# Two cross-attentions over one context: low halves on other engines, more buffers, and four tiles turned by the DMA queue

## The chip, the cores and the metric

The kernel runs on one core of one Trainium2 chip, in one launch. The metric is device time in microseconds; the three runs of the kernel before have a median of 407.05 us (406.81 to 407.90). A profiled execution is one more run, with its own time. The core has five engines, each with its own queue of instructions: TensorE (PE; PEld is its weight load), VectorE (DVE), ScalarE (ACT), GpSimd (POOL) and SyncE (SP), which here issues nearly all DMAs. They meet at semaphores.

## The reference

Two layers on 64 tokens of 128 features. Each layer begins with cross-attention (16 heads of 64) to one shared context of 6272 tokens; then follow small blocks: self-attention and a mixture of 8 experts in the first layer, a delta rule with FIR filters and gates and a quantised feed-forward in the second. Cut to what matters here:

```
x = x + xattn0(layernorm(x), ctx, mask)    # attention 1: scores masked, softmax over 6272 keys
x = x + attn0(layernorm(x));  x = x + moe(layernorm(x))
y = layernorm(x)
out = y + attn(q=y, k=ctx, v=ctx)          # attention 2: the same context, no mask
x = x + attn(q=out, k=out, v=y)            # small
x = x + delta(layernorm(x));  x = x + ffn_quantised(layernorm(x))

attn(q, k, v) = softmax(q Wq (k Wk)^T / 8) (v Wv) Wo      # per head
```

## The kernel before

The weights of keys and values are folded into the query and the output, so both attentions work on the raw context. A tile is 128 rows (2 heads x 64 tokens) by 896 keys; there are 8 row tiles (RT) and 7 chunks of keys (CH), so 56 tiles (STEPS) in each attention, numbered n = 0 to 55 chunk by chunk. The softmax runs online: a running maximum, and the sums U and den are rescaled by alpha from chunk to chunk. Precision comes from halves: each f32 operand is split into an upper f16 and a low f16 (the rest), and a product is three f16 matmuls.

One tile passes through these stations:

- TensorE: scores, six matmuls (`score`, L490), into one of two pairs of PSUM banks.
- VectorE: the scaled, masked row maximum and the tile itself into `probs` (`maximum`, L641), one of 4 slots; slot n % 4 is free again when tile n - 4 has its low half (or has been turned by TensorE).
- ScalarE: the exponential with its row sums (`exps`, L559), then the upper half into a slot of `halves` (`upper`, L566). The upper half of tile n comes behind the exponential of tile n + 1.
- VectorE or GpSimd: the low half, `probs` minus upper half (`lower`, L594). `on_vector(L, n)` says which; L is 0 in attention 1 and 1 in attention 2.
- SyncE: a DMA transpose of both halves, 128 x 1792 f16, into a slot of `probsT` (`turn`, L421). It waits for the low half, and for the product of tile n - BUFS.
- TensorE: the product with the context, 21 matmuls (`pv`, L522), PV_LAG = 5 steps behind.
- VectorE: the sum into U (`add`, L654), ADD_LAG = 6 steps behind.

Some tiles take another way (`on_pe`): TensorE turns `probs` in f32 into PSUM (L502, 7 transposes), ScalarE copies the upper halves out (L573, L575) and VectorE the low ones (L661). Before, these are in attention 1 the tiles n % 4 = 3 from 7 on, and in both attentions tiles 51, 53, 54 and 55.

The order of the work is written out by hand, engine by engine. TensorE's step i is the scores of tile i + 2, a turn of tile i - 1 if that is its own, the product of tile i - 5. VectorE's step i is the maximum of tile i, the low half of tile i - 2 if that is VectorE's, the low half of a turned tile i - 3, and the sum of tile i - 6. GpSimd takes its low halves in order of n, and between them in attention 1 the next chunks of the context (scaled, split) and their mask, in attention 2 the quantisation of the feed-forward weights, one step every fourth tile from 12 to 40; and at n % 8 = 1 the running denominators. SyncE issues in order of n; in attention 1 a context transpose comes after every eighth tile (n % 8 = 3), and after the tiles named in WEIGHTS_AT a load of weights for later stages. SyncE issues in order: whatever waits in front holds up what is behind.

`dma_index` counts the tiles that go by DMA; their slot of `halves` is that index modulo HALF_BUFS, and each slot has a semaphore of its own. The tile `probsT` has BUFS slots, `halves` HALF_BUFS.

Of the kernel before, what the change touches and what calls it, by code (L numbers as in the profile page):

```python
# [19 lines left out]
P = 128  # L20
# [9 lines left out]
CK = TC * P  # L30
# [106 lines left out]
def build(nc, dram):  # L137
    with ExitStack() as ctx:
# [82 lines left out]
        probsT_parts = probsT[:].rearrange("p b k -> p (b k)").bitcast(F16).rearrange("p (b h k) -> p b h k", b=4, h=2)  # L221
        negmax = sb("negmax", [P, (CH + 1) * RT])
# [166 lines left out]
        def _(sp):  # L389
# [24 lines left out]
            def turn(L, n):  # L414

                if on_pe(L, n):
                    return
                sp.wait_ge(*lower_of(L, n))
                if n >= BUFS:
                    sp.wait_ge(sem("pv_done"), L * STEPS + n - BUFS + 1)  # L420
                sp.dma_start_transpose(probsT_parts[:, n % BUFS, :, :].rearrange("p h (k r) -> p (h k) r", r=P),  # L421
                                       halves_of(L, n).rearrange("p h k -> p (h k)")).then_inc(turned(L, n)[0], 16)
# [37 lines left out]
        def flash_pe(pe, L):  # L460
# [47 lines left out]
            def pv(n):  # L508
                c, b, bank = n // RT, n % BUFS, PV_BANKS[n % len(PV_BANKS)]
# [40 lines left out]
        def flash_act(act, L):  # L550
# [17 lines left out]
            def turned_upper(n):  # L568
                k = pe_index(L, n)
                act.wait_ge(sem("p_turned_lo"), k + 1)  # L570
                if n >= BUFS:
                    act.wait_ge(sem("pv_done"), base + n - BUFS + 1)
                act.copy(probsT_parts[:, n % BUFS, 0, 0:4 * P], ps[:, turn_banks(n)[0], :]).then_inc(sem("p_upper"), 1)  # L573
                act.wait_ge(sem("p_turned_hi"), k + 1)
                act.copy(probsT_parts[:, n % BUFS, 0, 4 * P:CK],  # L575
                         ps[:, turn_banks(n)[1], 0:CK - 4 * P]).then_inc(sem("p_upper"), 1)
# [43 lines left out]
        def flash_dve(dve, L, aside={}):  # L620
# [37 lines left out]
            def turned_lower(n):  # L658
                for part, (a, w) in enumerate(((0, 4 * P), (4 * P, CK - 4 * P))):
                    dve.wait_ge(sem("p_upper"), 2 * pe_index(L, n) + part + 1)  # L660
                    dve.tensor_tensor(probsT_parts[:, n % BUFS, 1, a:a + w], ps[:, turn_banks(n)[part], 0:w],  # L661
                                      probsT_parts[:, n % BUFS, 0, a:a + w], ALU.subtract).then_inc(sem("p_lower"), 1)
# [38 lines left out]
        def ctxT_first_dve(dve, half):  # L701

            dve.wait_ge(sem("ctxT_upper"), half + 1)
            keys = FIRST_KEYS[half]
            dve.scalar_tensor_tensor(ctxT_parts[:, CK + keys.start:CK + keys.stop], ctxT_raw[:, keys],
                                     ch_scale[:], ctxT_parts[:, keys], ALU.mult,
                                     ALU.subtract).then_inc(sem("ctxT_ready" if half else "ctxT_lower"), 1)

# [318 lines left out]
        def _(pe):  # L1027
# [39 lines left out]
            for half in range(2):  # L1067
                pe.wait_ge(sem("a_probs"), half + 1)
                for k in range(2):
# [6 lines left out]
            for half in range(2):  # L1076
                pe.wait_ge(sem("a_pcopied"), half + 1)
                for q in (half, 2 + half):
# [87 lines left out]
            for half in range(2):  # L1166
                pe.wait_ge(sem("b_probs"), half + 1)
                for k in range(2):
# [4 lines left out]
            for half in range(2):  # L1173
                pe.wait_ge(sem("b_pcopied"), half + 1)
                for a in range(2):
# [182 lines left out]
        def _(pool):  # L1358
# [129 lines left out]
        def _(act):  # L1488
# [19 lines left out]
            for half in range(2):  # L1508
                act.wait_ge(sem("a_max"), half + 1)
# [3 lines left out]
                ins.then_inc(sem("a_exp"), 1)  # L1513
            for half in range(2):
                act.wait_ge(sem("a_given"), A_GIVEN["pturned"] + half)
                act.copy(PT[:, 2 * half:2 * half + 2, :].rearrange("p j c -> p (j c)"),
                         ps[:, half, 0:2 * P]).then_inc(sem("a_pcopied"), 1)
            loaded(act, "par")
# [21 lines left out]
            for half in range(2):  # L1540
                act.wait_ge(sem("b_max"), half + 1)
# [3 lines left out]
                ins.then_inc(sem("b_exp"), 1)  # L1545
            for half in range(2):
                act.wait_ge(sem("b_pturned"), half + 1)
                act.copy(PT[:, 2 * half:2 * half + 2, :].rearrange("p j c -> p (j c)"),
                         ps[:, 4 + 3 * half, 0:2 * P]).then_inc(sem("b_pcopied"), 1)
            for half in range(2):  # L1550
# [49 lines left out]
        def _(dve):  # L1600
# [65 lines left out]
            for half in range(2):  # L1666
# [5 lines left out]
                seq(dve.scalar_tensor_tensor(sm2[:, rs, :], sm[:, rs, :], NEVER, sc, ALU.mult, ALU.add))  # L1672
                dve.tensor_reduce(smx[:, rs], sm2[:, rs, :], AX, ALU.max, negate=True).then_inc(sem("a_max"), 1)
            for half in range(2):
                rs = slice(4 * half, 4 * half + 4)
                dve.wait_ge(sem("a_exp"), half + 1)
                seq(dve.tensor_reduce(ssum[:, rs], sm[:, rs, :], AX, ALU.add))
                seq(dve.reciprocal(ssum[:, rs], ssum[:, rs]))
                dve.tensor_tensor(sm[:, rs, :], sm[:, rs, :], ssum[:, rs].unsqueeze(2).broadcast_to([P, 4, S]),
                                  ALU.mult).then_inc(sem("a_probs"), 1)  # L1680
            seq(dve.tensor_scalar(wamx[:], wamx[:], 1e-8, None, ALU.max))
# [94 lines left out]
            for half in range(2):  # L1776
                dve.wait_ge(sem("b_scores"), half + 1)
                dve.tensor_reduce(smx[:, 4 * half:4 * half + 4],
                                  ps[:, 3 - half, 0:4 * S].rearrange("p (h t) -> p h t", h=4), AX, ALU.max,
                                  negate=True).then_inc(sem("b_max"), 1)  # L1780
            for half in range(2):
                rs = slice(4 * half, 4 * half + 4)
                dve.wait_ge(sem("b_exp"), half + 1)
                seq(dve.tensor_reduce(ssum[:, rs], sm[:, rs, :], AX, ALU.add))
                seq(dve.reciprocal(ssum[:, rs], ssum[:, rs]))
                dve.tensor_tensor(sm[:, rs, :], sm[:, rs, :], ssum[:, rs].unsqueeze(2).broadcast_to([P, 4, S]),
                                  ALU.mult).then_inc(sem("b_probs"), 1)
            for half in range(2):
# [227 lines left out]
```

## Time and profile before

| | |
|---|---|
| median of three runs | 407.05 us |
| the profiled execution | 407.44 us, span 405.6 us, mean granted clock 0.995 |
| PE busy | 383.4 us (95%) |
| DVE, ACT busy | 286.4 us (71%), 287.9 us (71%) |
| POOL busy | 237.8 us (59%) |
| SyncE's DMA queue | 188048 packets, 66.77 MB, 81.7% of 16 engines |
| attention 1, attention 2 | about 19 to 172 us, about 210 to 351 us |

In the rows below L490 is a line of the kernel, `probsT<-halves` what is written and read, and x the count. A busy PE is a modelled one: matmuls are pipelined and the end of one lies behind the start of the next. The time in brackets is how long the engine stood idle before the row, and what ended that. SyncE's rows (SPq) are the issue of a DMA; its landing comes later. Times count from the start of the span.

### The profile page before, as it was taken

What the parts mean: (1) busy time and instruction counts of PE and PEld (TensorE: products, weight loads), DVE (VectorE), ACT (ScalarE), POOL (GpSimd) and SP (SyncE); (2) the same over time, 40 slices, a digit from 0 to 9 for tenths busy, and PEclk for the clock granted to TensorE, in tenths of its full rate; (3) what the DMA queues carried; (4) which work ended last, traced back from release to release, by engine and by line L of the source; (5) the groups of instructions that cost most, each with busy time, mean ns of one, the idle gap of its engine ahead of it and who ended that gap; (6) DMA issues with size and microseconds to landing.
All of it is one profiled execution on the core that took longest, in us unless ns stands there. A gap on an engine that the chain in (4) does not pass through costs nothing.

```text
span 405.6 us, 11389 instructions
## 1 busy us (share of the span) xinstructions
PE 383.4 (95%) x4529; PEld 280.3 (69%) x4529; DVE 286.4 (71%) x724; ACT 287.9 (71%) x568; POOL 237.8 (59%) x198
## 2 busy tenths in 40 slices
PE   7988999999998999989999999999999999999996
PEld 3435777777776778964955767777777778867843
DVE  2788888888875777556667767887887776445544
ACT  3477888888787887737429988899889987534240
POOL 2388989999974559301006997887787659030000
PEclk9899999999999999999999999999999999999999
DMA  8899998979989997990004999999999999700000
GB/s 307 321 257 193 178 179 136 178 143 210 238 179 212 190 210 137 331 410 34 3 2 90 193 192 194 193 201 192 206 170 210 183 206 185 284 2 2 4 1 5
DMA packets 188390, 68.56 MB, mean 169 GB/s; under 512 B 183200, under 2 KB 183984, under 8 KB 187440
## 3 DMA queue, kind: packets, MB, share of 16 engines
q1 hardware_dynamic: 188048, 66.77, 81.7%
q10 hardware_dynamic: 288, 1.05, 0.8%
q8 instruction: 36, 0.59, 0.6%
q14 instruction: 18, 0.15, 0.1%
HBM read 21.90 MB, written 0.03 MB: 54 GB/s over the span
## 4 chain that ended last, share of the span: by engine, by line
PE 52%; DVE 16%; DMA 10%; POOL 7%; ACT 6%; issue 6%; SPq 2%; POOLq 0%; DVEq 0%; ACTq 0%
PE ps L522 18%; PE ps L490 14%; DMA probsT<-halves 8%; DVE probs L641 7%; POOL halves L594 5%; PE ps L502 3%; ACT probs L559 2%; PE ps L1104 2%; PE ps L766 2%; SPq L421 2%; DMA moe<-in_ctxT 2%; ACT halves L566 1%; DVE U L654 1%; PE ps L1212 1%; PE ps L826 1%
## 5 line engine op out<-in xcount | busy, mean ns | idle before, releaser
L594 POOL TENSOR_TENSOR halves<-probs,halves 128x896 f16<-128x896 f32 x75 | 141.6, 1892 | 54.9 <-ACT halves L566 53.5
L522 PE MATMUL ps<-ctxN,probsT 128*128 128x128 f16 x2352 | 148.6, 219 | 4.6 <-DMA probsT<-halves 3.6
L522 PEld LDWEIGHTS ps<-ctxN,probsT 128*128 128x128 f16 x2352 | 139.4, 98 | 18.1 <-issue 8.0
L490 PE MATMUL ps<-ctxT_parts,GT_parts 128*128 128x512 f16 (+1 forms) x660 | 143.0, 353 | 5.4 <-DVE negmax L641 5.3
L559 ACT ACTIVATE probs<-probs,shifted 128x896 f32<-128x896 f32 x112 | 115.5, 1031 | 6.5 <-DVE shifted L646 6.5
L490 PEld LDWEIGHTS ps<-ctxT_parts,GT_parts 128*128 128x128 f16 x660 | 59.6, 98 | 57.0 <-DVE negmax L641 8.1
L566 ACT CAST halves<-probs 128x896 f16<-128x896 f32 x93 | 85.8, 923 | 0.1
L654 DVE SCALAR_TENSOR_TENSOR U<-U,alpha,ps 128x128 f32<-128x128 f32 x112 | 38.6, 345 | 54.4 <-PE ps L522 54.1
L641 DVE CUSTOM_DVE_ANT_0 probs<-ps,zero,negmax 128x896 f32<-128x896 f32 x56 | 67.5, 1205 | 1.7 <-POOL halves L594 1.2
L641 DVE CUSTOM_DVE_ANT_0 probs<-ps,maskb,negmax 128x896 f32<-128x896 f32 x56 | 67.5, 1205 | 1.6 <-issue 0.7
L556 ACT ACTIVATE alpha<-negmax 128x1 f32<-128x1 f32 x96 | 28.2, 294 | 37.0 <-DVE negmax L641 36.3
L766 PE MATMUL ps<-cst 128*128 128x512 f16 x135 | 34.8, 380 | 0.0
L594 DVE TENSOR_TENSOR halves<-probs,halves 128x896 f16<-128x896 f32 x18 | 24.0, 1336 | 0.7 <-ACT halves L566 0.7
L661 DVE TENSOR_TENSOR probsT<-ps,probsT 128x512 f16<-128x512 f32 (+1 forms) x38 | 21.8, 616 | 3.6 <-ACT probsT L573 3.6
L761 POOL TENSOR_TENSOR rstd<-mv,pows 128x1 f32<-128x1 f32 (+1 forms) x6 | 3.3, 546 | 35.1 <-DVE mv L745 24.1
L766 PEld LDWEIGHTS ps<-cst 128*128 128x128 f16 x135 | 13.0, 100 | 11.7 <-issue 0.9
L559 ACT ACTIVATION_READ_ACCUMULATOR probs<-probs,shifted 128x1 f32 x112 | 20.9, 187 | 0.0
L646 DVE TENSOR_SCALAR shifted<-negmax 128x1 f32<-128x1 f32 x112 | 17.2, 154 | 3.9
L502 PE MATMUL ps<-cst,probs 128*128 128x128 f32 x133 | 17.3, 273 | 0.0
L1385 POOL TENSOR_SCALAR maskb<-moe 128x896 bf16<-128x896 int32 x5 | 16.1, 3217 | 0.4
L502 PEld LDWEIGHTS ps<-cst,probs 128*128 128x128 f32 x133 | 15.3, 141 | 1.1
L1483 POOL TENSOR_TENSOR orn<-oms,pows 128x2 f32<-128x2 f32 x1 | 0.7, 698 | 23.3 <-DVE oms L1909 23.3
(369 smaller groups left out, 380.3 us busy)
## 6 DMA issues: line engine op xcount, KB each, us to landing
moe<-in_ctxT SPq DMA_DIRECT2D x7, 448.0 KB, 7.6
moe<-in_mask SPq DMA_DIRECT2D x6, 448.0 KB, 10.0
moe<-in_gateT SPq DMA_DIRECT2D x2, 1024.0 KB, 9.2
moe<-in_upT SPq DMA_DIRECT2D x2, 1024.0 KB, 10.9
moe<-in_downT SPq DMA_DIRECT2D x2, 1024.0 KB, 12.8
moe<-in_fir_long SPq DMA_DIRECT2D x1, 2048.0 KB, 10.3
probsT<-halves SPq DMA_TRANSPOSE x93, 4.6
wv<-in_wv SPq DMA_DIRECT2D x2, 512.0 KB, 6.9
```

What stands on the lines that cost most here:

```text
L490: ins = pe.matmul(ps[:, 2 * b + h, 0:width], GT_parts[:, g_part, r * P:(r + 1) * P], ctxT_parts[:, keys:keys + width], start=(g_part == 0 ...
L502: ins = pe.transpose(ps[:, turn_banks(n)[t // 4], t % 4 * P:(t % 4 + 1) * P], probs[:, n % BUFS, t * P:(t + 1) * P], ident)
L522: ins = pe.matmul(ps[:, bank, 0:D], probsT_parts[:, b, p_part, k * P:(k + 1) * P], ctxN_parts[:, at:at + D], start=(p_part == 0 and c_part ...
L556: act.activation(alpha[:, n:n + 1], negmax[:, n:n + 1], ACT.Exp, bias=negmax[:, n + RT:n + RT + 1], scale=-1.0)
L559: act.activation(probs[:, n % BUFS, :], probs[:, n % BUFS, :], ACT.Exp, bias=shifted[:, n:n + 1], scale=-1.0, accum_out=chunksum[:, n:n + ...
L566: act.copy(halves_of(L, n)[:, 0, :], probs[:, n % BUFS, :]).then_inc(sem("upper_done"), 1)
L594: eng.tensor_tensor(halves_of(L, n)[:, 1, :], probs[:, n % BUFS, :], halves_of(L, n)[:, 0, :], ALU.subtract).then_inc(lower_of(L, n)[0], 1)
L641: dve.tensor_tensor_reduce(out=probs[:, n % BUFS, :], in0=scored, in1=added, scale=descale[:, L:L + 1], scalar=negmax[:, n:n + 1], op0=ALU ...
L646: dve.tensor_scalar(shifted[:, n:n + 1], negmax[:, n + RT:n + RT + 1], PROB_LOG, None, ALU.add).then_inc(sem("shifted"), 1)
L654: dve.scalar_tensor_tensor(U[:, r, :], U[:, r, :], alpha[:, n:n + 1], ps[:, PV_BANKS[n % len(PV_BANKS)], 0:D], ALU.mult, ALU.add).then_inc ...
L661: dve.tensor_tensor(probsT_parts[:, n % BUFS, 1, a:a + w], ps[:, turn_banks(n)[part], 0:w], probsT_parts[:, n % BUFS, 0, a:a + w], ALU.sub ...
L766: pe.matmul(ps[:, bank, :], ident.bitcast(F16)[:, 0:P], cst[:, 0:2 * P].bitcast(F16), start=True, stop=True)
```

## The change

Of the fifteen tiles that TensorE turns in attention 1, four (35, 39, 43 and 47) now go by DMA. In attention 1 VectorE makes the low halves of tile 0 and of n % 4 = 1 up to 33 (tile 2 goes to GpSimd, tile 33 comes from it), and from tile 5 on one step later than before: behind the maximum of tile n + 3 instead of n + 2. In attention 2 all low halves are GpSimd's; before, nine were VectorE's (n % 4 = 3 from 15 to 47). `probsT` has 6 slots instead of 4, `halves` 7 instead of 5; the room comes from a descriptor scratch of 1024 bytes in place of the default. Loads of weights stand at other tiles. Semaphores of two small blocks are shared (a_... and b_... become s_..., the second block counting on), and one unused increment goes.

```diff
-BUFS, HALF_BUFS = 4, 5
+BUFS, TURNED_BUFS, HALF_BUFS = 4, 6, 7
-RAMP = 12
...
-        probsT = sb("probsT", [P, BUFS, CK])
+        probsT = sb("probsT", [P, TURNED_BUFS, CK])
...
-        WEIGHTS_AT = {24: ("in1", w_qT, "wqT1"), 27: ("in1", wkT[:], "wkT1"), 30: ("out0", wv[:], "wv0"),
-                      33: ("out0", wo[:], "wo0"), 36: ("ffn", win[:], "win"), 38: ("ffn", wout[:], "wout"),
-                      40: ("small_attn", a_w[:], "a_w"), 42: ("delta", d_w[:], "d_w"), 44: ("delta", w1s[:], "w1s")}
+        WEIGHTS_AT = {14: ("in1", w_qT, "wqT1"), 22: ("in1", wkT[:], "wkT1"), 30: ("out0", wv[:], "wv0"),
+                      34: ("small_attn", a_w[:], "a_w"), 36: ("ffn", win[:], "win"), 38: ("out0", wo[:], "wo0"),
+                      40: ("ffn", wout[:], "wout"), 44: ("delta", d_w[:], "d_w"), 46: ("delta", w1s[:], "w1s")}
 
         def on_pe(L, n):
-            return L == 0 and n % 4 == 3 and n > 4 or n >= STEPS - 3 or n == STEPS - 5
+            return L == 0 and n % 4 == 3 and 4 < n < 33 or n >= STEPS - 3 or n == STEPS - 5
 
         def on_vector(L, n):
             if L == 0:
-                return n in (0, 2) or 4 <= n < 30 and n % 4 == 1
-            return n >= RAMP and n % 4 == 3
+                return n == 0 or 4 <= n < 34 and n % 4 == 1
+            return False
...
-                if n >= BUFS:
-                    sp.wait_ge(sem("pv_done"), L * STEPS + n - BUFS + 1)
+                if n >= TURNED_BUFS:
+                    sp.wait_ge(sem("pv_done"), L * STEPS + n - TURNED_BUFS + 1)
...
-                if 2 <= i < STEPS + 2 and on_vector(L, i - 2) and not on_pe(L, i - 2):
-                    lower(dve, L, i - 2)
+                done = i - (2 if L or i <= 4 else 3)
+                if (0 if L or i <= 4 else BUFS) <= done < STEPS and on_vector(L, done) and not on_pe(L, done):
+                    lower(dve, L, done)
...
-    nc = bacc.Bacc("TRN2", target_bir_lowering=False, num_devices=1)
+    nc = bacc.Bacc("TRN2", target_bir_lowering=False, num_devices=1, dynamic_dma_scratch_size=1024)
```

## Rows read from the trace of the kernel before

**Rows 1.** The page: span, SyncE's queue, and a transpose's issue to landing (last column, us).
```profile
span 405.6 us, 11389 instructions
...
q1 hardware_dynamic: 188048, 66.77, 81.7%
...
probsT<-halves SPq DMA_TRANSPOSE x93, 4.6
```
**Rows 2.** Stages: length, busy PE, PEld, DVE, ACT, POOL, PEclk, DMA share, GB/s.
```profile
117.22:149.80 32.58, 30.78 (x358) 24.04 (x356) 23.27 (x57) 26.61 (x55) 18.25 (x12) 1.00 1.17 211
224.24:336.11 111.87, 109.49 (x1266) 82.15 (x1265) 86.47 (x197) 99.62 (x187) 88.02 (x65) 1.00 1.17 195
```
**Rows 3.** TensorE's order in attention 1: start, us, instruction, count, [idle before].
```profile
108.43 1.30 PE L490 MATMUL ps<-ctxT_parts,GT_parts 128*128 128x512 f16 x6
...
110.74 1.30 PE L490 MATMUL ps<-ctxT_parts,GT_parts 128*128 128x512 f16 x6
...
123.83 1.33 PE L522 MATMUL ps<-ctxN,probsT 128*128 128x128 f16 x21 [1.80 <-DMA probsT<-halves]
125.00 1.30 PE L490 MATMUL ps<-ctxT_parts,GT_parts 128*128 128x512 f16 x6
...
128.07 1.30 PE L490 MATMUL ps<-ctxT_parts,GT_parts 128*128 128x512 f16 x6
...
162.71 1.70 PE L502 MATMUL ps<-cst,probs 128*128 128x128 f32 x14
```
**Rows 4.** Waits of TensorE, 36-105, 105-160, 211-352 us: us, times, longest.
```profile
PE ps L490 <- DVE negmax L641: 2.3, 5, 1.0
...
PE ps L522 <- DMA probsT<-halves: 1.8, 1, 1.8
...
PE ps L522 <- DMA probsT<-halves: 1.8, 5, 0.6
...
PE ps L490 <- DVE negmax L641: 0.4, 1, 0.4
```
**Rows 5.** SyncE's order in attention 1: start, us of the issue.
```profile
115.61 1.10 SPq L391 DMA_DIRECT2D wo<-in_wo  x1
117.22 1.56 SPq L421 DMA_TRANSPOSE probsT<-halves  x1
118.82 3.21 SPq L411 DMA_TRANSPOSE ctxN<-ctxT_parts  x1
122.13 2.99 SPq L421 DMA_TRANSPOSE probsT<-halves  x1
```
**Rows 6.** Issues in attention 2, 224 to 336.2 us: ns min/median/max, first and last.
```profile
L421 SPq DMA_TRANSPOSE probsT<-halves x48: 1297/2094/3612, 224.2 to 336.1; - x48
```
**Rows 7.** GpSimd's order in attention 2.
```profile
220.45 9.35 POOL L594 TENSOR_TENSOR halves<-probs,halves 128x896 f16<-128x896 f32 x5 [1.00 <-ACT halves L566]
...
251.75 1.90 POOL L594 TENSOR_TENSOR halves<-probs,halves 128x896 f16<-128x896 f32 x1 [2.51 <-ACT halves L566]
...
255.64 1.89 POOL L594 TENSOR_TENSOR halves<-probs,halves 128x896 f16<-128x896 f32 x1
```
**Rows 8.** Two short stretches of attention 2, columns as in rows 2.
```profile
218.75:220.50 1.75, 1.75 (x10) 0.87 (x9) 1.55 (x4) 1.75 (x4) 0.75 (x2) 1.00 1.13 214
...
239.50:241.00 1.50, 1.50 (x25) 1.33 (x23) 0.91 (x3) 0.71 (x2) 1.50 (x2) 1.00 1.26 280
```
**Rows 9.** GpSimd's and VectorE's order before tile 34's issue.
```profile
108.82 3.22 POOL L1385 TENSOR_SCALAR maskb<-UT 128x896 bf16<-128x896 int32 x1
112.11 1.90 POOL L594 TENSOR_TENSOR halves<-probs,halves 128x896 f16<-128x896 f32 x1
...
111.20 1.21 DVE L641 CUSTOM_DVE_ANT_0 probs<-ps,maskb,negmax 128x896 f32<-128x896 f32 x1
```
**Rows 10.** VectorE's low halves, both attentions: ns min/median/max, first and last.
```profile
L594 DVE TENSOR_TENSOR halves<-probs,halves x18: 1080/1106/2581, 26.2 to 325.5; 128x896 f16<-128x896 f32 x18
```
**Rows 11.** Waits of SyncE, 205 to 355 us.
```profile
SPq L420 <- PE ps L522: 0.2, 1, 0.2
```

More of the change, by code:

```diff
@@ L218, in build @@
         scrap = probs[:, 2:4, :].rearrange("p b k -> p (b k)")
-        probsT = sb("probsT", [P, BUFS, CK])
+        probsT = sb("probsT", [P, TURNED_BUFS, CK])
         halves = sb("halves", [P, HALF_BUFS, 2, CK], F16)
-        probsT_parts = probsT[:].rearrange("p b k -> p (b k)").bitcast(F16).rearrange("p (b h k) -> p b h k", b=4, h=2)
+        probsT_parts = probsT[:].rearrange("p b k -> p (b k)").bitcast(F16).rearrange("p (b h k) -> p b h k", b=TURNED_BUFS,
+                                                                                      h=2)
         negmax = sb("negmax", [P, (CH + 1) * RT])
@@ L418, in turn @@
                 sp.wait_ge(*lower_of(L, n))
[L419 to L421 removed]
+                if n >= TURNED_BUFS:
+                    sp.wait_ge(sem("pv_done"), L * STEPS + n - TURNED_BUFS + 1)
+                sp.dma_start_transpose(probsT_parts[:, n % TURNED_BUFS, :, :].rearrange("p h (k r) -> p (h k) r", r=P),
                                        halves_of(L, n).rearrange("p h k -> p (h k)")).then_inc(turned(L, n)[0], 16)
@@ L508, in pv @@
             def pv(n):
-                c, b, bank = n // RT, n % BUFS, PV_BANKS[n % len(PV_BANKS)]
+                c, b, bank = n // RT, n % TURNED_BUFS, PV_BANKS[n % len(PV_BANKS)]
                 if L == 0 and n % RT == 0:
@@ L570, in turned_upper @@
                 act.wait_ge(sem("p_turned_lo"), k + 1)
-                if n >= BUFS:
-                    act.wait_ge(sem("pv_done"), base + n - BUFS + 1)
-                act.copy(probsT_parts[:, n % BUFS, 0, 0:4 * P], ps[:, turn_banks(n)[0], :]).then_inc(sem("p_upper"), 1)
+                if n >= TURNED_BUFS:
+                    act.wait_ge(sem("pv_done"), base + n - TURNED_BUFS + 1)
+                act.copy(probsT_parts[:, n % TURNED_BUFS, 0, 0:4 * P], ps[:, turn_banks(n)[0], :]).then_inc(sem("p_upper"), 1)
                 act.wait_ge(sem("p_turned_hi"), k + 1)
-                act.copy(probsT_parts[:, n % BUFS, 0, 4 * P:CK],
+                act.copy(probsT_parts[:, n % TURNED_BUFS, 0, 4 * P:CK],
                          ps[:, turn_banks(n)[1], 0:CK - 4 * P]).then_inc(sem("p_upper"), 1)
@@ L660, in turned_lower @@
                     dve.wait_ge(sem("p_upper"), 2 * pe_index(L, n) + part + 1)
-                    dve.tensor_tensor(probsT_parts[:, n % BUFS, 1, a:a + w], ps[:, turn_banks(n)[part], 0:w],
-                                      probsT_parts[:, n % BUFS, 0, a:a + w], ALU.subtract).then_inc(sem("p_lower"), 1)
+                    dve.tensor_tensor(probsT_parts[:, n % TURNED_BUFS, 1, a:a + w], ps[:, turn_banks(n)[part], 0:w],
+                                      probsT_parts[:, n % TURNED_BUFS, 0, a:a + w], ALU.subtract).then_inc(sem("p_lower"), 1)
             for i in range(STEPS + ADD_LAG):
@@ L704, in ctxT_first_dve @@
             keys = FIRST_KEYS[half]
-            dve.scalar_tensor_tensor(ctxT_parts[:, CK + keys.start:CK + keys.stop], ctxT_raw[:, keys],
-                                     ch_scale[:], ctxT_parts[:, keys], ALU.mult,
-                                     ALU.subtract).then_inc(sem("ctxT_ready" if half else "ctxT_lower"), 1)
+            ins = dve.scalar_tensor_tensor(ctxT_parts[:, CK + keys.start:CK + keys.stop], ctxT_raw[:, keys],
+                                           ch_scale[:], ctxT_parts[:, keys], ALU.mult, ALU.subtract)
+            if half:
+                ins.then_inc(sem("ctxT_ready"), 1)
         def bound_dve(dve, seq, L, total):
@@ L1067, in _ @@
             for half in range(2):
-                pe.wait_ge(sem("a_probs"), half + 1)
+                pe.wait_ge(sem("s_probs"), half + 1)
                 for k in range(2):
@@ L1076, in _ @@
             for half in range(2):
-                pe.wait_ge(sem("a_pcopied"), half + 1)
+                pe.wait_ge(sem("s_pcopied"), half + 1)
                 for q in (half, 2 + half):
@@ L1166, in _ @@
             for half in range(2):
-                pe.wait_ge(sem("b_probs"), half + 1)
+                pe.wait_ge(sem("s_probs"), half + 3)
                 for k in range(2):
@@ L1173, in _ @@
             for half in range(2):
-                pe.wait_ge(sem("b_pcopied"), half + 1)
+                pe.wait_ge(sem("s_pcopied"), half + 3)
                 for a in range(2):
@@ L1452, in _ @@
                     pool.wait_ge(sem("u_turned"), 3)
-                    pool.wait_ge(sem("a_max"), 2)
+                    pool.wait_ge(sem("s_max"), 2)
                     pool.memset(den[:], 0.0).then_inc(sem("cleared"), 1)
@@ L1508, in _ @@
             for half in range(2):
-                act.wait_ge(sem("a_max"), half + 1)
+                act.wait_ge(sem("s_max"), half + 1)
                 for k in range(4):
@@ L1512, in _ @@
                     ins = act.activation(sm[:, r, :], sm2[:, r, :], ACT.Exp, bias=smx[:, r:r + 1])
-                ins.then_inc(sem("a_exp"), 1)
+                ins.then_inc(sem("s_exp"), 1)
             for half in range(2):
@@ L1516, in _ @@
                 act.copy(PT[:, 2 * half:2 * half + 2, :].rearrange("p j c -> p (j c)"),
-                         ps[:, half, 0:2 * P]).then_inc(sem("a_pcopied"), 1)
+                         ps[:, half, 0:2 * P]).then_inc(sem("s_pcopied"), 1)
             loaded(act, "par")
@@ L1540, in _ @@
             for half in range(2):
-                act.wait_ge(sem("b_max"), half + 1)
+                act.wait_ge(sem("s_max"), half + 3)
                 for k in range(RT // 2):
@@ L1544, in _ @@
                     ins = act.activation(sm[:, r, :], ps[:, 3 - half, k * S:(k + 1) * S], ACT.Exp, bias=smx[:, r:r + 1])
-                ins.then_inc(sem("b_exp"), 1)
+                ins.then_inc(sem("s_exp"), 1)
             for half in range(2):
@@ L1548, in _ @@
                 act.copy(PT[:, 2 * half:2 * half + 2, :].rearrange("p j c -> p (j c)"),
-                         ps[:, 4 + 3 * half, 0:2 * P]).then_inc(sem("b_pcopied"), 1)
+                         ps[:, 4 + 3 * half, 0:2 * P]).then_inc(sem("s_pcopied"), 1)
             for half in range(2):
@@ L1672, in _ @@
                 seq(dve.scalar_tensor_tensor(sm2[:, rs, :], sm[:, rs, :], NEVER, sc, ALU.mult, ALU.add))
-                dve.tensor_reduce(smx[:, rs], sm2[:, rs, :], AX, ALU.max, negate=True).then_inc(sem("a_max"), 1)
+                dve.tensor_reduce(smx[:, rs], sm2[:, rs, :], AX, ALU.max, negate=True).then_inc(sem("s_max"), 1)
             for half in range(2):
                 rs = slice(4 * half, 4 * half + 4)
-                dve.wait_ge(sem("a_exp"), half + 1)
+                dve.wait_ge(sem("s_exp"), half + 1)
                 seq(dve.tensor_reduce(ssum[:, rs], sm[:, rs, :], AX, ALU.add))
@@ L1679, in _ @@
                 dve.tensor_tensor(sm[:, rs, :], sm[:, rs, :], ssum[:, rs].unsqueeze(2).broadcast_to([P, 4, S]),
-                                  ALU.mult).then_inc(sem("a_probs"), 1)
+                                  ALU.mult).then_inc(sem("s_probs"), 1)
             seq(dve.tensor_scalar(wamx[:], wamx[:], 1e-8, None, ALU.max))
@@ L1779, in _ @@
                                   ps[:, 3 - half, 0:4 * S].rearrange("p (h t) -> p h t", h=4), AX, ALU.max,
-                                  negate=True).then_inc(sem("b_max"), 1)
+                                  negate=True).then_inc(sem("s_max"), 1)
             for half in range(2):
                 rs = slice(4 * half, 4 * half + 4)
-                dve.wait_ge(sem("b_exp"), half + 1)
+                dve.wait_ge(sem("s_exp"), half + 3)
                 seq(dve.tensor_reduce(ssum[:, rs], sm[:, rs, :], AX, ALU.add))
@@ L1786, in _ @@
                 dve.tensor_tensor(sm[:, rs, :], sm[:, rs, :], ssum[:, rs].unsqueeze(2).broadcast_to([P, 4, S]),
-                                  ALU.mult).then_inc(sem("b_probs"), 1)
+                                  ALU.mult).then_inc(sem("s_probs"), 1)
             for half in range(2):
```

## The prediction

> **What bounds the kernel now.** I read the page first, then the stages, then TensorE's and the DMA queue's own order, then the waits. The page [rows 1] has a span of 405.6 us, of which SyncE's queue, which carries nearly all transfers, fills 82% of the 16 engines. The stages [rows 2] show where: in attention 2 (224 to 336 us) and in 117 to 150 us of attention 1 the queue's share is 1.17, above 1 since packets overlap. The granted clock is 1.00 in both (the upper level, 2.4 GHz), so nothing is lost there. In TensorE's order [rows 3] a step is 2.31 us (108.43 to 110.74: the scores of one tile and the product of another), and 3.07 us when TensorE turns a tile as well (125.00 to 128.07); a turn is 0.77 us. The stage is TensorE's wherever nothing else is late, and the reader is to see what is late in the waits [rows 4]: in attention 1 VectorE's row maximum up to 105 us (five waits), then one late DMA tile, 1.80 us before 123.83 [rows 3]; in attention 2 almost only late DMA tiles. The queue's order [rows 5] shows why: from tile 34's issue at 117.22 on, each issue begins 0.04 to 0.1 us after the one before has ended. In attention 2 there are 48 issues from 224.2 to 336.1 [rows 6], one per (336.1 - 224.2) / 47 = 2.38 us, at the pace of TensorE. So two things bound attention in turns, TensorE and the queue, and the change takes work from the first and gives it to the second.
>
> **The change, part by part.** All sums are made against the profiled execution, 407.44 us, of which 405.6 are the span; the median of the runs, 407.05, lies 0.39 lower.
>
> *Four turns leave TensorE* (tiles 35, 39, 43 and 47 of attention 1). TensorE loses 4 x 0.77 = 3.1 us. ScalarE's two copies and VectorE's two subtractions for each go too; neither engine releases TensorE in that stretch [rows 4], so I count nothing. GpSimd gets four low halves of 1.87 us (9.35 us for five in a row, [rows 7]); behind tile 34 it has 2.31 us per tile and little else, so they are hidden.
>
> *The queue gets four tiles*, each 128 x 1792 two-byte elements, 0.459 MB. What it does from tile 34's issue on, before: ten tiles, two context transposes and five loads in 32.6 us (117.22 to 149.8), without a pause [rows 2, 5]. After: the same, three more tiles (35, 39, 43) up to the issue of tile 47, and the load of wo0, which moves from tile 33 to tile 38 and takes 1.10 us to issue [rows 5]; then tiles 47 to 49 until tile 50 is issued. With t for a tile more in a full queue that is 32.6 + 1.1 + 6t. Bounds for t: 0.459 MB at 280 GB/s, the best rate of a stretch, is 1.6 us, and at the 195 GB/s of all of attention 2 it is 2.35 us; one transpose alone runs at 214 GB/s, 2.1 us [rows 2, 8]. That is the nearest row; as a backlog can speed it up, I take 2.0. To the issue of tile 50: 45.7 us. Landing is 4.6 us after the issue [rows 1], 0.1 until TensorE starts and 1.2 for the product: 51.6 us from tile 34's issue to the end of tile 50's product. Before, that product ends where the turns of tiles 53 and 54 begin, at 162.71: 162.71 - 117.22 = 45.5 us [rows 3, 5]. So this stretch grows by 6.1 us (3.7 to 8.2). TensorE alone would want, from product to product, 16 x 2.31 + 0.77 = 37.7 us; the queue wants about 8 us more, and the 3.1 us saved are lost in waits.
>
> The Trainium skill, "DMA: Bandwidth & Descriptors", section "Latency and other measured facts", gives a DMA transpose an effective 261 GB/s. Nineteen transposes and 1.64 MB of loads are 10.4 MB, 39.7 us by that figure as an estimate, against 49 us at the 211 GB/s of rows 2; by the page the queue would hold TensorE by some 2 us and not 8, and the first rival would win. The trace has a rate like it only in short stretches [rows 8].
>
> *Low halves one step later in attention 1* (VectorE's tiles, n % 4 = 1). They move from the step before a turn into the one with the turn, which is 0.77 us longer. The five waits for the maximum, 2.3 us [rows 4], mostly go; a modelled end lies 0.16 us behind the next start (123.83 + 1.33 against 125.00, [rows 3]), so from start to start they are 3.1 us. The longest, 1.0 + 0.16 near tile 8, I count as given back: tile 2's low half goes to GpSimd, behind a mask conversion like that of 3.22 us in rows 9, and the issues of tiles 2, 3 and 4 move back with it. That leaves 1.9; I take 1.7 us (0.8 to 3.1), and by so much tile 34's step comes earlier. A tile's low half lands about 2 us later in the queue; the tiles have more than that in hand up to tile 32, where the queue is not full.
>
> *Where tile 34's issue comes.* Before, at 117.22: a mask, then the low half of tile 33 on GpSimd at 112.11 and of tile 34 behind it, then wo0 [rows 5, 9]. After: tile 33's low half is VectorE's, behind the maximum of tile 36, which began at 111.20 [rows 9] and now 1.7 earlier, at 109.5; it ends 1.4 later, the subtraction takes 1.1 to 2.6 us [rows 10], since GpSimd starts tile 34's at the same moment; tile 33's issue of 1.5 us follows. Tile 34 is issued at 113.6 to 115.1; I take the middle, 2.9 earlier than before. Attention 1 so ends 6.1 - 2.9 = 3.2 us later. Bounds: 3.7 - 2.9 - 0.8 = 0 and 8.2 - 2.0 = 6.2.
>
> *All low halves on GpSimd in attention 2.* VectorE loses nine, and the one wait of 0.4 us for the maximum [rows 4] goes. GpSimd, tiles 12 to 43: 32 x 1.87 = 59.8; eight steps of the weight quantisation, each pushing the next low half back by 1.0 to 2.1 us (255.64 - 251.75 = 3.89, so 2.0 more, [rows 7]; all eight 12.4); four running denominators, 2.0, one copy, 0.8. Sum 75.0 us, against 32 x 2.31 = 73.9 for TensorE. So GpSimd becomes as tight as the other two. Its lag is largest, about 3.3 us, behind the second weight's third step (tile 37). A low half may be late by 1.5 us before the maximum four tiles on waits for it, and that by 0.6 before TensorE does: up to 1.2 us in all, less what TensorE loses anyway on late DMA tiles (1.8 us, rows 4), in which GpSimd catches up. I take +0.7, with the 0.4 gained +0.3 (-0.6 to +2.0).
>
> *Deeper buffers.* In attention 2 the queue's waits on the product four tiles back sum to 0.2 us, once [rows 11]; what it waits for there is the low half. So six and seven slots instead of four and five give 0 (0 to 0.2). A tile whose low half is late gains nothing by a free slot.
>
> *The smaller descriptor scratch* makes room for them. Every transpose here is issued by SyncE. No row shows what the scratch does. The Trainium skill, "DMA: Bandwidth & Descriptors", section "SWDGE vs HWDGE vs iDMA", says that the rings in that carveout serve DMAs issued by GpSimd and that SyncE's path does not touch them; no run here shows it. I take 0. The merged semaphores and the dropped increment change no order: 0. Loads: wqT1 and wkT1 move to tiles 14 and 22, where the queue has pauses: 0, and it costs about 1 us of issue each if that cover is gone.
>
> Sum: 405.6 + 3.2 + 0.3 = 409.1 us of span; with the 1.84 us around it 410.9, and by the 0.39 of the median 410.5 us.
>
> **Rivals.**
> 1. *The queue has room (faster).* If a full queue runs at its best rate (280 GB/s, rows 8) for longer, each of 19 transposes takes 1.6 us, the loads hide among them, and TensorE bounds attention 1: from tile 34's product to tile 50's 37.7 us, which starts 5 steps after the step at 108.43 - 1.7. Product 50 would end at 158.3 instead of 162.71, -4.4, and with +0.3 the time is 403.0. For it: the rate has been seen, and before 117 us the queue paused. Against it: the 32.6 us in which it never paused ran at 211 GB/s.
> 2. *Balance.* t is 1.6 and tile 34 comes early (113.6): 3.7 - 2.9 - 0.8 = 0 in attention 1, and 407.3 in all.
> 3. *GpSimd bounds attention 2.* Attention 1 even, but the lag of 3.3 us meets the late DMA tiles instead of hiding in them: 1.2 us and 0.2 more for each of the five waits, less 0.4: +1.8, 408.9.
> 4. *It doesn't do what it says:* the smaller scratch slows every transpose. At the longest issue seen, 3.6 us [rows 6], instead of 2.1, 97 transposes cost over 100 us.
>
> **How the numbers follow.** Forecast 0.48; rival 1 0.25; rival 2 0.17; rival 3 0.07; rival 4 0.03. A run of this kernel can tell 0.3%, 1.2 us. Faster (below 405.8) is rival 1: 0.25. Same is rival 2: 0.17. Slower is the forecast with rivals 3 and 4: 0.58. The forecast alone runs from 408.3 to 413. The range of 8 in 10 reaches into rival 1 until half of it is left out, 404.5, and up to 413.0.
>
> **What would show it.** After: late DMA tiles as TensorE's largest wait between 118 and 162 us, some 8 us, where there was one of 1.8; SyncE's issues without a pause from tile 34 to tile 50, tile 50 issued near 160; 4 x 7 transposes fewer at L502; no wait of TensorE for the maximum up to 105 us but the first. In attention 2 no low half on VectorE, GpSimd without a pause between tiles 16 and 44, late DMA tiles about as before. I am wrong if the issues of tiles 34 to 50 follow each other in under 2.2 us on the mean, loads included, or if attention 2 changes by more than 2 us.

## The result and the profile after

The changed kernel takes 415.74 us (median of 4 runs, 415.21 to 416.06), against 407.48 for the kernel before, run beside it: ratio 1.0198, 95% interval 1.0177 to 1.0219. It is slower, as forecast, but by 8.3 us where 3.4 were forecast, and it lies above the range (404.5 to 413.0). The profiled execution took 415.80.

The page of the changed kernel: the span, TensorE's turns, the DMA queue, and the transposes' issue to landing.
```profile
span 413.7 us, 11323 instructions
...
L502 PE MATMUL ps<-cst,probs 128*128 128x128 f32 x105 | 13.6, 273 | 0.0
...
q1 hardware_dynamic: 195344, 68.61, 83.1%
...
probsT<-halves SPq DMA_TRANSPOSE x97, 4.8
```
105 transposes on TensorE are 15 tiles, four fewer than before, and the queue has 97 transposes instead of 93 [rows 1]. So the change does what it says.

SyncE's order in the changed kernel, from tile 34's issue on, and the issues of tiles 44 and 50 (columns as in [rows 5], the last one a count):
```profile
115.94 1.78 SPq L421 DMA_TRANSPOSE probsT<-halves  x1
117.77 1.08 SPq L391 DMA_DIRECT2D a_w<-in_a_w  x1
119.36 1.92 SPq L421 DMA_TRANSPOSE probsT<-halves  x1
121.34 2.66 SPq L411 DMA_TRANSPOSE ctxN<-ctxT_parts  x1
124.10 1.56 SPq L421 DMA_TRANSPOSE probsT<-halves  x1
...
126.88 3.89 SPq L421 DMA_TRANSPOSE probsT<-halves  x2
130.83 1.06 SPq L391 DMA_DIRECT2D wo<-in_wo  x1
131.98 5.25 SPq L421 DMA_TRANSPOSE probsT<-halves  x2
...
147.52 3.31 SPq L421 DMA_TRANSPOSE probsT<-halves  x1
...
163.28 5.32 SPq L421 DMA_TRANSPOSE probsT<-halves  x2
```
Up to tile 50 each issue follows the one before within 0.15 us, but for the 0.51 behind the first load. Tile 34 is issued at 115.94 (117.22 before, [rows 5]) and tile 50 at 163.28.

TensorE's order in the changed kernel: three early waits, the scores of tile 36 and the end of product 50 as in [rows 3], and the longest wait between them.
```profile
35.39 1.31 PE L490 MATMUL ps<-ctxT_parts,GT_parts 128*128 128x512 f16 x6 [1.63 <-DVE negmax L641]
...
44.84 1.33 PE L522 MATMUL ps<-ctxN,probsT 128*128 128x128 f16 x21 [0.46 <-DMA probsT<-halves]
...
48.10 1.33 PE L522 MATMUL ps<-ctxN,probsT 128*128 128x128 f16 x21 [0.79 <-DMA probsT<-halves]
...
108.08 1.30 PE L490 MATMUL ps<-ctxT_parts,GT_parts 128*128 128x512 f16 x6
...
139.18 1.53 PE L522 MATMUL ps<-ctxN,probsT 128*128 128x128 f16 x21 [3.08 <-DMA probsT<-halves]
...
169.64 1.70 PE L502 MATMUL ps<-cst,probs 128*128 128x128 f32 x14
```
The row at 108.08 (the scores of tile 36) stood at 108.43 before; the turns of tiles 53 and 54, which begin when the product of tile 50 ends, stand at 169.64 instead of 162.71: 6.9 us later. That is most of the 8.1 us that the span grew by.

TensorE's waits in the changed kernel (us, times, longest), from 28 to 120, 120 to 178 and 218 to 360 us:
```profile
PE ps L490 <- DVE negmax L641: 2.7, 3, 1.6
PE ps L522 <- DMA probsT<-halves: 1.8, 3, 0.8
...
PE ps L522 <- DMA probsT<-halves: 8.4, 8, 3.1
...
PE ps L522 <- DMA probsT<-halves: 4.1, 10, 0.8
PE ps L490 <- DVE GT_parts L881: 0.2, 1, 0.2
```
Against [rows 4]: late DMA tiles cost 8.4 us in the second half of attention 1, where there was one wait of 1.8; and the first half has waits of its own. In attention 2 they cost 4.1 instead of 1.8.

It is the queue that is late there, and not GpSimd, which now makes the low halves of all these tiles. GpSimd's row for tile 44's low half:
```profile
138.75 1.88 POOL L594 TENSOR_TENSOR halves<-probs,halves 128x896 f16<-128x896 f32 x1 [0.43 <-ACT halves L566]
```
It ends at 140.63, and SyncE issues tile 44 at 147.52. From tile 35 to tile 50 each low half ends 1.6 to 7.2 us before its tile is issued. The stretch of the full queue, columns as in [rows 2]:
```profile
115.94:163.28 47.34, 40.49 (x441) 29.48 (x440) 26.27 (x65) 34.70 (x66) 33.49 (x26) 0.96 1.13 209
```
The transposes of attention 2, as in [rows 6]:
```profile
L421 SPq DMA_TRANSPOSE probsT<-halves x48: 1342/2033/3833, 230.9 to 343.8; - x48
```
The rate is 209 GB/s where it was 211. In attention 2 the 48 issues span 112.8 us instead of 111.9.

### The profile page after: what moved, and what is told of

It is laid out like the page before. It is cut to its first block, busy times and chain, and to the rows that moved or that the text cites. A ratio compares the mean times of both kernels' runs of the same rounds, so it can differ in the third digit from the quotient of the medians.

```text
span 413.7 us, 11323 instructions
## 1 busy us (share of the span) xinstructions
PE 382.5 (92%) x4501; PEld 277.0 (67%) x4501; DVE 273.1 (66%) x707; ACT 287.8 (70%) x564; POOL 263.8 (64%) x211
## 4 chain that ended last, share of the span: by engine, by line
PE 44%; POOL 15%; DMA 15%; DVE 10%; ACT 7%; issue 5%; SPq 2%; POOLq 0%; DVEq 0%; ACTq 0%
PE ps L522 16%; DMA probsT<-halves 13%; PE ps L490 12%; POOL halves L594 11%; DVE probs L641 3%; ACT probs L559 2%; DMA moe<-in_ctxT 2%; ACT halves L566 2%; PE ps L1106 2%; PE ps L502 2%; PE ps L768 2%; PE ps L1214 1%; PE ps L828 1%; PE ps L942 1%; DVE halves L594 1%
## 5 line engine op out<-in xcount | busy, mean ns | idle before, releaser
L594 POOL TENSOR_TENSOR halves<-probs,halves 128x896 f16<-128x896 f32 x88 | 168.3, 1922 | 34.5 <-ACT halves L566 33.2
L566 ACT CAST halves<-probs 128x896 f16<-128x896 f32 x97 | 89.5, 923 | 0.1
L661 DVE TENSOR_TENSOR probsT<-ps,probsT 128x512 f16<-128x512 f32 (+1 forms) x30 | 17.3, 618 | 6.1 <-ACT probsT L573 6.1
L502 PE MATMUL ps<-cst,probs 128*128 128x128 f32 x105 | 13.6, 273 | 0.0
L594 DVE TENSOR_TENSOR halves<-probs,halves 128x896 f16<-128x896 f32 x9 | 12.8, 1419 | 0.0
L502 PEld LDWEIGHTS ps<-cst,probs 128*128 128x128 f32 x105 | 12.0, 141 | 0.8
```

Source lines behind the costliest of these rows:

```text
L502: ins = pe.transpose(ps[:, turn_banks(n)[t // 4], t % 4 * P:(t % 4 + 1) * P], probs[:, n % BUFS, t * P:(t + 1) * P], ident)
L566: act.copy(halves_of(L, n)[:, 0, :], probs[:, n % BUFS, :]).then_inc(sem("upper_done"), 1)
L594: eng.tensor_tensor(halves_of(L, n)[:, 1, :], probs[:, n % BUFS, :], halves_of(L, n)[:, 0, :], ALU.subtract).then_inc(lower_of(L, n)[0], 1)
L661: dve.tensor_tensor(probsT_parts[:, n % TURNED_BUFS, 1, a:a + w], ps[:, turn_banks(n)[part], 0:w], probsT_parts[:, n % TURNED_BUFS, 0, a:a ...
```

## The experiments

**Which part costs.** Four kernels, each one part undone or one part alone.

a_turns_back: the changed kernel with TensorE's tiles as before.
```diff
-            return L == 0 and n % 4 == 3 and 4 < n < 33 or n >= STEPS - 3 or n == STEPS - 5
+            return L == 0 and n % 4 == 3 and n > 4 or n >= STEPS - 3 or n == STEPS - 5
```


> The changed kernel, but TensorE turns tiles 35, 39, 43 and 47 of attention 1 again. Theory Q (the queue is full from tile 34 to tile 50 and each of the four tiles costs it some 2.3 us): the 8.4 us that TensorE waits for late DMA tiles between 120 and 178 us fall under 2, the product of tile 50 ends near 161.5 us instead of 169.7, attention 2 keeps its 1.4 us more, and the time is 407.3 us (before: 407.5; changed: 415.7). Rival S (every transpose became slower through the smaller scratch, the more slots or the moved loads): the late tiles stay, four turns of 0.77 us come on top, and the time is 412 us or more.

Measured: 406.95 us, ratio to before 0.9984 (0.9967 to 1.0). No late DMA tile from 105 us to the end of attention 1; product 50 ends at:
```profile
160.75 1.70 PE L502 MATMUL ps<-cst,probs 128*128 128x128 f32 x14
```

b_four_only: the kernel before with that one line as in the changed kernel (the diff above, read backwards).

> The kernel before, but tiles 35, 39, 43 and 47 of attention 1 go by DMA; nothing else of the change. Theory Q: from tile 34's issue at 117.2 us the queue takes 32.6 + 6 x 2.27 = 46.2 us to the issue of tile 50, whose product ends near 169.3 us, 6.6 later than before: 414.1 us. Rival S (the four tiles fit, and it is the scratch, the slots or the loads that cost): 406 to 408.5 us.

Measured: 415.55 us, 1.0199 (1.0171 to 1.0227); late DMA tiles, 115 to 178 us, and the end of product 50:
```profile
PE ps L522 <- DMA probsT<-halves: 7.1, 5, 2.4
```
```profile
169.04 1.16 PE L502 MATMUL ps<-cst,probs 128*128 128x128 f32 x9
```
The four tiles alone make the whole difference, and taking them back takes the whole difference away. Rival S falls: from tile 34's issue (116.95) to tile 50's (162.99) b needs 46.0 us with four and five slots, the default scratch and five loads; the changed kernel needs 47.3 with six and seven slots, the small scratch and six loads.

c_att2_vector and d_att1_lows_back: the changed kernel with the low halves of attention 2, or those of attention 1, as before.
```diff
 c:
-            return False
+            return n >= 12 and n % 4 == 3
 d:
-                return n == 0 or 4 <= n < 34 and n % 4 == 1
+                return n in (0, 2) or 4 <= n < 30 and n % 4 == 1
...
-                done = i - (2 if L or i <= 4 else 3)
-                if (0 if L or i <= 4 else BUFS) <= done < STEPS and on_vector(L, done) and not on_pe(L, done):
+                done = i - 2
+                if 0 <= done < STEPS and on_vector(L, done) and not on_pe(L, done):
```


> The changed kernel, but VectorE makes nine low halves of attention 2 again (n % 4 = 3 from 15 to 47). Theory G (GpSimd as the only maker of low halves leaves the queue waiting, which costs the 1.4 us by which attention 2 grew): the last product of attention 2 starts 140.0 us after its first scores, as before, and not 141.3; time 414.4 us. Rival I (the 1.4 us are an accident of which transposes fall on a pause of the queue): still about 141.3, time 415.7 us.

> The changed kernel, but the low halves of attention 1 are made as before: tiles 0, 2 and n % 4 = 1 from 5 to 29 by VectorE, tile 33 by GpSimd, none a step later. Theory L (the later low halves are what brought tile 34's issue forward from 117.2 to 115.9 us, and it decides when the full queue starts): tile 34 is issued near 117.2 again, time 417.0 us. Rival E (what the new assignment costs at the start, 4.2 us of waits up to step 15 where there were 1.6, with tiles 2 to 5 late, is more than it gives): tile 34 is issued at 115 or before, time 413.5 to 415 us.

Measured: c 416.06 us (1.0212, 1.0185 to 1.0239), though its attention 2 took 140.1 us from first scores to last product, as G expected; d 416.26 us (1.0214, 1.0188 to 1.0241), with tile 34 issued at 116.18. Neither gain nor loss shows in the times: G is not borne out, and L and E both miss. The moved loads alone give d's start (116.24 in g_loads_only below), so next to nothing of the changed kernel's earlier start comes from its low halves. That they neither gained nor lost in sum asked for the run on tile 2 below.

**What a tile and a load cost the full queue.** e_loads_later and h_two_tiles, both on the changed kernel (the last two lines of e stand behind the loop over the tiles of attention 1):
```diff
 e:
...
-                      34: ("small_attn", a_w[:], "a_w"), 36: ("ffn", win[:], "win"), 38: ("out0", wo[:], "wo0"),
-                      40: ("ffn", wout[:], "wout"), 44: ("delta", d_w[:], "d_w"), 46: ("delta", w1s[:], "w1s")}
+        WEIGHTS_LAST = [("out0", wo[:], "wo0"), ("small_attn", a_w[:], "a_w"), ("ffn", win[:], "win"),
+                        ("ffn", wout[:], "wout"), ("delta", d_w[:], "d_w"), ("delta", w1s[:], "w1s")]
...
+            for name, t, src in WEIGHTS_LAST:
+                load(name, t, src)
 h:
-            return L == 0 and n % 4 == 3 and 4 < n < 33 or n >= STEPS - 3 or n == STEPS - 5
+            return L == 0 and n % 4 == 3 and 4 < n < 41 or n >= STEPS - 3 or n == STEPS - 5
```


> The changed kernel, but the six loads of weights that stand behind tiles 34 to 46 of attention 1 come behind all its tiles. Theory Q (in the full queue everything costs by its bytes: a transpose some 2.28 us, a load about 1.05): from tile 34's issue to tile 50's 18 transposes remain, 18 x 2.28 = 41.0 us instead of 47.3; the product of tile 50 ends near 163.4 us instead of 169.7, and the time is 409.4 us. Rival W (loads ride in gaps between the transposes for nothing, and a transpose costs 47.3 / 18 = 2.6 us): 47 us as before, 415.5 us. By the 2.0 us a tile of the prediction it would be 36 us, TensorE would bound, and 406 us come out.

> The changed kernel, but TensorE turns tiles 35 and 39 again; 43 and 47 stay with the DMA queue. Theory Q (full queue, 2.28 us a tile): 47.3 - 4.6 = 42.8 us from tile 34's issue to tile 50's, product 50 ends near 165 us, time 411 us, half-way between 407.0 with four turns back and 415.7. Rival T (the queue has room for two tiles, and it only tips over with four): 406.5 to 408 us.

Measured: e 411.09 us (1.0076, 1.0049 to 1.0103). SyncE's order in e, between the issues of tiles 34 and 50, and the rate of that stretch:
```profile
116.50 3.72 SPq L421 DMA_TRANSPOSE probsT<-halves  x2
120.27 3.61 SPq L411 DMA_TRANSPOSE ctxN<-ctxT_parts  x1
123.99 17.75 SPq L421 DMA_TRANSPOSE probsT<-halves  x8
141.79 2.19 SPq L411 DMA_TRANSPOSE ctxN<-ctxT_parts  x1
144.07 14.30 SPq L421 DMA_TRANSPOSE probsT<-halves  x6
```
```profile
116.50:158.46 41.96, 37.93 (x435) 28.07 (x433) 25.84 (x64) 33.88 (x65) 33.24 (x26) 1.00 1.17 196
```
18 transposes in 41.96 us, nothing between them: 2.33 us each, and TensorE still waits for late tiles. The six loads cost 47.34 - 41.96 = 5.4 us, 0.9 each (by the times 4.7, 0.8 each); theory W falls. e comes out 1.7 us above what Q expected: 1.0 in this stretch, the rest in a later start and in attention 2.

h: 410.99 us (1.0081, 1.006 to 1.0101), where Q expected 411 and T at most 408: two tiles cost 4.0 us above a_turns_back, and two more 4.8. The queue has no room for even two. But in its profile the stretch took 45.4 us, not 42.8. In the five profiles with all four tiles and the loads between them (the changed kernel, b, c, d, i) it took 46.0 to 47.6, so by the stretch two tiles fewer take off 1 to 2 us where Q has 4.6. Only the times agree with Q; why the stretch does not stays open.

**Where the earlier start went.** i_tile2_back: the changed kernel with tile 2's low half by VectorE.
```diff
-                return n == 0 or 4 <= n < 34 and n % 4 == 1
+                return n in (0, 2) or 4 <= n < 34 and n % 4 == 1
```


> The changed kernel with one low half moved back: tile 2 of attention 1 by VectorE. Theory M (tile 2's low half behind GpSimd's first mask is what ate the gain of the later low halves, so that the full queue starts only at 115.9 us): the scores of tile 36 start near 106.2 us instead of 108.1, tile 34 is issued near 114 us, the product of tile 50 ends near 167.7 us, and the time is 413.7 us. Rival K (before tile 34 the queue is already so late that an earlier TensorE gains nothing): 415.5 us.

Measured: 412.98 us (1.0145, 1.0122 to 1.0168): by this one low half 2.8 us less than the changed kernel, or 2.2 by the two ratios, each to the kernel before run beside it. TensorE's order in i:
```profile
32.81 1.31 PE L490 MATMUL ps<-ctxT_parts,GT_parts 128*128 128x512 f16 x6 [1.14 <-DVE negmax L641]
...
105.52 1.30 PE L490 MATMUL ps<-ctxT_parts,GT_parts 128*128 128x512 f16 x6
...
165.95 1.70 PE L502 MATMUL ps<-cst,probs 128*128 128x128 f32 x14
```
The scores of tile 36 start at 105.52, 2.6 us before those of the changed kernel, tile 34 is issued at 112.98, 3.0 before, and product 50 ends 3.7 earlier. Other profiles bear it out: with tile 2 on VectorE these scores start at 105.3 to 106.2 (i, and f, j and k below; l, whose attention 1 began late, is left aside), with tile 2 on GpSimd at 108.1 to 108.6 (the changed kernel, a, c, e, h). What tile 2 does there is in the changed kernel's GpSimd and VectorE:
```profile
28.79 3.22 POOL L1387 TENSOR_SCALAR maskb<-moe 128x896 bf16<-128x896 int32 x1
32.09 5.58 POOL L594 TENSOR_TENSOR halves<-probs,halves 128x896 f16<-128x896 f32 x3
```
```profile
34.12 1.21 DVE L641 CUSTOM_DVE_ANT_0 probs<-ps,maskb,negmax 128x896 f32<-128x896 f32 x1 [3.09 <-POOL halves L594]
```
Tile 2's low half waits for the mask conversion, and tiles 3 and 4 come behind it. VectorE's maximum of tile 6 needs the slot of tile 2 and stands 3.09 us; TensorE loses 1.63 for it, and 0.46 and 0.79 for the late transposes of tiles 4 and 5 (rows of TensorE above).

g_loads_only: the kernel before with the loads at the changed places.

> The kernel before with the loads of weights at the changed places, nothing else. Theory O (wo0 in front of tile 34 made its DMA late, 1.96 us of TensorE's wait): tile 34 is issued 1.1 us earlier, the wait falls under 0.9 us, time 406.3 us. Rival N (a load moved behind tile 38 makes a later tile late by as much): 407.5 us.

Measured: 406.50 us, 0.9979 (0.9965 to 0.9993). Tile 34 is issued at 116.24, one wait for a late tile is left between 110 and 178 us:
```profile
PE ps L522 <- DMA probsT<-halves: 0.6, 1, 0.6
```
The moved loads are worth about 1 us, and with wo0 out of its way tile 34 is issued 1.0 earlier, as O expected.

**What is good in the change, and the version that beats both.** f_parts is a_turns_back with c's line and i's line; j_gpsimd_att2 is f without c's line; k_few_slots is f with the slots and the scratch of before:
```diff
 k:
-BUFS, TURNED_BUFS, HALF_BUFS = 4, 6, 7
+BUFS, TURNED_BUFS, HALF_BUFS = 4, 4, 5
...
-    nc = bacc.Bacc("TRN2", target_bir_lowering=False, num_devices=1, dynamic_dma_scratch_size=1024)
+    nc = bacc.Bacc("TRN2", target_bir_lowering=False, num_devices=1)
```


> The changed kernel with three parts undone: TensorE turns all its tiles again, VectorE makes nine low halves of attention 2 again, and that of tile 2 of attention 1. Theory R (what is left, later low halves from tile 5 on, the moved loads and more slots, gains, and the two low-half assignments lose): the scores of tile 36 start near 106.5 us instead of 108.1, attention 2 takes 140.2 us instead of 141.0, and the time is 404.5 us. Rival Z (the early waits only move, as with the other assignment, and attention 2's difference is within its scatter): 406.5 to 407 us.

> The same kernel as f_parts, beside the two that each differ from it in one part: 404.7 us.

> f_parts, but all low halves of attention 2 are GpSimd's. Theory G (GpSimd alone is as tight as the queue there and starves it now and then): 0.8 us more than f_parts, 405.5 us; the last product starts 141.1 us after the first scores of attention 2 instead of 140.3. Rival I (scatter): 404.7 us.

> f_parts with four slots of probsT, five of halves and the default descriptor scratch, as before. Theory N (more slots and the smaller scratch do nothing, since the queue waits for low halves and not for slots): 404.7 us. Rival D (with four slots the queue waits for products in attention 1, some 11 us in 8 waits before, and a late tile stays late): 405.5 to 406.5 us.

| | us (range) | ratio to before |
|---|---|---|
| f_parts | 404.74 (403.98 to 405.37) | 0.9931 (0.9905 to 0.9957) |
| l_parts_again | 405.13 (403.94 to 408.29) | 0.9935 (0.9914 to 0.9957) |
| j_gpsimd_att2 | 404.65 (403.63 to 404.97) | 0.9931 (0.991 to 0.9952) |
| k_few_slots | 404.12 (403.32 to 405.34) | 0.9921 (0.9898 to 0.9943) |

The highest run, l's 408.29, is its profiled execution, in which TensorE's granted clock over the first 20 us was 0.74 (0.91 in f's); its attention 1 began 3.3 us later. In f the scores of tile 36 start at 106.16 and product 50 ends at 158.50, with no late DMA tile in between (the row between them is the product of tile 34):
```profile
106.16 1.30 PE L490 MATMUL ps<-ctxT_parts,GT_parts 128*128 128x512 f16 x6
...
119.60 1.33 PE L522 MATMUL ps<-ctxN,probsT 128*128 128x128 f16 x21
...
158.50 1.70 PE L502 MATMUL ps<-cst,probs 128*128 128x128 f32 x14
```
R's time is right, by attention 1 alone: attention 2 of f took 141.1 us where R expected 140.2, against the changed kernel's 141.3. j and l do not differ, so all low halves on GpSimd cost nothing that these times can show. k and l do not differ by more than their intervals: more slots and the smaller scratch do nothing that the times show, and D falls. Every version that keeps the four turns on TensorE, the later low halves and the moved loads, and leaves tile 2 to VectorE, is 0.7 to 0.8% faster than the kernel before, and so faster than the changed one too. j differs from a_turns_back in tile 2's low half alone: 0.9931 against 0.9984.

## Why the prediction was wrong

The mechanism was right: the queue is full from tile 34 on, four tiles more make TensorE wait for late DMA tiles (some 8 us expected, 8.4 measured), the saved turns are lost in them. That 8 and 8.4 agree is in part luck: the 37.7 us of TensorE alone, from product 34 to product 50, count scores in the last two of these steps, which have none (2 x 1.13 us). f needs these 37.7 us with three turns more (119.60 to 158.50, less 1.2 for the last product), so the sum should have had 35.4, and the queue's excess was 10. The forecast does not use this number.

Two terms of the forecast's sum were mis-sized, both in the same direction. Of the 4.9 us by which it fell short, 3.7 lie before the end of product 50 and 1.1 in attention 2 of the two profiles. Against the forecast, product 50 ends 3.7 us later (169.64 for 162.71 + 3.2 = 165.9):

- **Tile 34's issue, forecast 114.3, came at 115.94: 1.6 us.** The step that failed is "The longest, 1.0 + 0.16 near tile 8, I count as given back". It saw that tile 2's low half on GpSimd stands behind a mask, but priced it as the return of one known wait. It costs 2.6 us up to tile 36 (i_tile2_back). With it undone the scores of tile 36 come 2.9 us earlier than before (108.43 to 105.52; 2.3 to 3.1 over i, f, j and k), nearly all of it by the later low halves, as the moved loads alone give 0.2; that is inside the 0.8 to 3.1 given. With it the gain is 0.35. The prediction's sign for it, no wait for the maximum but the first, did not come: there were three from 28 us on, the longest 1.6.
- **The price of a tile in a full queue, t = 2.0: 1.6 us.** From tile 34's issue to tile 50's there were 47.34 us instead of 45.7, so t = (47.34 - 32.6 - 1.1) / 6 = 2.27, within the bounds (1.6 to 2.35) but near their upper end; e_loads_later gives 2.33 for a transpose by itself. The failed step is the choice, "as a backlog can speed it up, I take 2.0". The rows held the answer: the 32.6 us of [rows 2] were twelve transposes and five loads, and even with each load at wo0's 1.10 us [rows 5] (32.6 - 5.5) / 12 = 2.26; with 0.9, as e measured it, 2.34.
- **Tile 50's landing: 0.5 us.** From its issue to the end of its product 6.4 us instead of 5.9.

The bounds of attention 1 (0 to 6.2) had been joined so that a high t met an early start; both came out on the bad side.

*Attention 2* was forecast 0.3 longer. In the two profiles it is 1.4 longer, but the runs do not support a cost of the change: with all low halves on GpSimd or nine on VectorE the times are alike (404.65 against 405.13; 415.74 against 416.06). Over the profiles it took 139.6 to 141.4 us with VectorE's part and 140.2 to 141.9 without, seven profiles each, with means of 140.5 and 141.2. Whether these tenths are real stays open; the forecast of no more than 0.3 stands as far as the times can tell.

*Slots and scratch* were counted 0: k_few_slots against l_parts_again, and b_four_only against the changed kernel, bear that out. The Trainium skill, "DMA: Bandwidth & Descriptors", section "SWDGE vs HWDGE vs iDMA", has it that the descriptor rings in the carveout serve GpSimd's DMAs and that SyncE's never touch them; the alike pace of b and the changed kernel agrees with it.

*Moved loads* were counted 0 for wqT1 and wkT1, and wo0 within the start of tile 34; g_loads_only, 1 us faster, fits.

*Rival 1* had the queue at 280 GB/s. The changed kernel's full queue ran at 209, e's transposes alone at 196: the best rate of a stretch of 1.5 us was no rate of 40 us. The traces show where such a rate stands: behind a pause of the queue, in the kernel before in front of the 280 GB/s of [rows 8]:
```profile
238.70:239.30 0.60, 0.60 (x5) 0.27 (x3) 0.52 (x2) 0.60 (x1) 0.60 (x1) 1.00 0.08 8
```
and in the changed kernel's full queue, while the transposes of tiles 39 and 40 were out:
```profile
137.30:138.60 1.30, 0.00 (x0) 0.00 (x0) 0.00 (x0) 1.30 (x3) 1.02 (x1) 1.00 0.19 8
138.70:139.70 1.00, 0.52 (x10) 0.55 (x11) 0.00 (x0) 0.00 (x0) 0.95 (x1) 1.00 1.26 285
```
In both places the queue moves 8 GB/s for a while and 280 to 285 right after; the mean of a long stretch holds both. What makes it pause was not tested by a run. The 261 GB/s that the Trainium skill gives in "DMA: Bandwidth & Descriptors", "Latency and other measured facts", for a transpose with a non-contiguous middle dimension, is not reached in any full stretch here. f's product 50 ends at 158.50, near the 158.3 of rival 1, but this is an accident: f keeps the four turns on TensorE, and rival 1's sum has the two steps' scores too many.

## What to carry to other kernels

Before work moves from one engine to a queue, count what the queue does in a stretch without a pause, item by item, and price one more item by that count, not by the best stretch or by one item alone: here TensorE's step was 2.31 us, a transpose in the full queue 2.33, and the four tiles cost 8 us more than their turns, which had cost 3. An operation that is moved behind a longer one of another engine at the start of a pipeline, as tile 2's low half here, can delay all that comes after, until some stage has room to take it up. Undo a change one part at a time: two of its parts, the later low halves and the moved loads, were worth 0.7% together, hidden behind tile 2's low half, which cost some 0.5%, and the four tiles, which cost 2%.

## What the runs showed of the hardware

After TensorE had stood 3.08 us for tile 39's transpose, its granted clock fell to the lower level. The changed kernel's windows (columns as in [rows 2]) and TensorE's order there:
```profile
140.50:142.00 1.50, 1.50 (x6) 0.60 (x5) 1.25 (x2) 0.00 (x0) 0.13 (x1) 0.50 1.33 158
...
144.00:145.00 1.00, 1.00 (x13) 0.65 (x11) 0.48 (x2) 0.41 (x1) 0.51 (x1) 1.00 0.57 119
```
```profile
140.51 2.44 PE L490 MATMUL ps<-ctxT_parts,GT_parts 128*128 128x512 f16 x6
142.75 1.74 PE L522 MATMUL ps<-ctxN,probsT 128*128 128x128 f16 x21
144.32 1.30 PE L490 MATMUL ps<-ctxT_parts,GT_parts 128*128 128x512 f16 x6
```
0.50 is 1.2 GHz: the scores took 2.44 us instead of 1.30 and the product 1.74 instead of 1.33. It does not add to the sum: the queue stays full through it (tile 45's low half still ends 5.2 us before its issue), and TensorE waits again for tiles 44 and 45. So a wait on the queue brought a slower clock with it here, which shows as busy time.
